# The last stage of a batch, done chunk by chunk inside the scan stage of the next batch

## The reference

```
# layer 0: dilated convolutions, batch norm, relu, then linear attention over the N = 16384 pixels
out = gamma * (msum * tailor)                 # per batch: a 17-row matrix u, and out = G^T u

# layer 1, with x_hsi the output of layer 0
xz = x @ W_in; xh, z = split(xz)              # 128 -> 2 x 256
xh = silu(causal_conv_k2(xh, conv_w, conv_b))
dt_low, Bmat, Cmat = split(xh @ W_x)          # 8 + 16 + 16
dt = softplus(dt_low @ W_dt + b_dt)
h  = exp(dt * A) * h + dt * B * x             # a scan over the pixels, 256 x 16 states
y  = (sum_n h * C + xh * D) * silu(z)
x  = y @ W_out                                # back to 128 channels: "o" below
x  = silu(group_norm(x, gamma, beta))         # 4 groups of 32 channels, over the whole image
return x + x_hsi
```

## Time and profile before

| | us |
|---|---|
| median of 3 runs (16718.77 to 16725.19) | 16720.4 |
| the profiled execution, its own time | 16713.74 |
| its span, first to last instruction | 16712.0 |
| busy: PE / DVE / ACT / POOL | 14237.2 / 14036.9 / 9963.5 / 13059.7 |
| granted TensorE clock, mean | 0.912 |

### The profile page before, as it was taken

One profiled execution on the slowest core, in us unless ns is written; L12 is line 12 of the kernel. 1 busy time (PEld: TensorE's weight loads), 2 busy tenths in 40 slices (PEclk: granted clock), 3 DMA queues, 4 the chain that ended last, 5 costly groups with the idle time before them and its releaser, 6 DMA issues. The chain is left out here.

```text
span 16712.0 us, 141790 instructions
## 1 busy us (share of the span) xinstructions
PE 14237.2 (85%) x40250; PEld 5369.3 (32%) x40250; DVE 14036.9 (84%) x13540; ACT 9963.5 (60%) x13655; POOL 13059.7 (78%) x5647
## 2 busy tenths in 40 slices
PE   8999988888888888888888888888888888888876
PEld 3333333333333333333333333333333333333322
DVE  1222229999999999999999999999999999999942
ACT  2222226666666666666666666666666666666631
POOL 0000009999999999999999999999999999999930
PEclk9999988999999999999999999999999999999965
DMA  1111104444444444444444444444444444444455
GB/s 49 42 44 38 39 27 167 166 169 169 166 169 169 169 166 166 166 167 162 167 168 169 169 166 169 169 166 169 167 167 162 166 167 167 169 169 167 168 194 211
DMA packets 508713, 2504.88 MB, mean 150 GB/s; under 512 B 53097, under 2 KB 164938, under 8 KB 226651
## 3 DMA queue, kind: packets, MB, share of 16 engines
q1 hardware_dynamic: 489723, 2419.71, 40.0%
q10 hardware_dynamic: 18208, 76.11, 1.2%
HBM read 2325.05 MB, written 170.57 MB: 149 GB/s over the span
## 5 line engine op out<-in xcount | busy, mean ns | idle before, releaser
L728 POOL TENSOR_TENSOR hc<-h,c_all 128x1024 f32<-128x1024 f32 x4096 | 9523.5, 2357 | 458.0 <-DVE h L1043 441.6
L940 PE MATMUL y_ps<-hc,ident 128*128 128x512 f32 x16392 | 8513.9, 665 | 1436.1 <-POOL hc L728 1434.1
L824 ACT ACTIVATE d_a<-dt,a_neg 128x512 f32<-128x512 f32 x8194 | 5594.9, 689 | 4215.2 <-DVE h L1043 4205.6
L1043 DVE TENSOR_TENSOR_SCAN h<-d_a,h,dbx_v 128x512 f32<-128x512 f32 x5456 | 6623.6, 1262 | 8.8
L940 PEld LDWEIGHTS y_ps<-hc,ident 128*128 128x128 f32 x16392 | 3304.4, 211 | 6533.9 <-issue 3802.1
L1030 DVE TENSOR_TENSOR dbx_v<-dtx_ps,b_all 128x1024 f32<-128x1024 f32 x2816 | 3316.3, 1208 | 60.3 <-DMA b_all<-bc_dram 24.4
L1043 DVE TENSOR_TENSOR_SCAN h<-d_a,h,dbx_p 128x512 f32<-128x512 f32 x2480 | 3024.4, 1261 | 0.0
L717 POOL TENSOR_TENSOR dbx_p<-dtx,b_all 128x1024 f32<-128x1024 f32 x1280 | 3000.2, 2353 | 25.0 <-DVE h L1043 2.0
L479 POOL MEMSET ident_f<- 128x128 f32 x1 | 0.2, 204 | 2416.7 <-POOLq L44 2416.7
L272 PE MATMUL conv_ps<-image,w_taps 128*32 128x512 f32 x11520 | 1778.8, 595 | 0.0
L362 DVE RECIPROCAL k_inv<-k_nrm 128x4 f32<-128x4 f32 x256 | 45.5, 178 | 1776.0 <-ACT k_nrm L214 1776.0
(11 more groups left out here) (123 smaller groups left out, 8958.7 us busy)
## 6 DMA issues: line engine op xcount, KB each, us to landing
b_all<-bc_dram SPq DMA_DIRECT2D x1028, 1024.0 KB, 6.3
c_all<-bc_dram SPq DMA_DIRECT2D x1025, 1024.0 KB, 4.8
o_dram<-o_sb SPq DMA_DIRECT2D x257, 256.0 KB, 5.6
o_t<-o_dram SPq DMA_DIRECT2D x64, 1024.0 KB, 11.0
out<-r_t ACTq DMA_DIRECT2D x64, 1024.0 KB, 9.2
image<-in_x SPq DMA_DIRECT2D x91, 512.0 KB, 4.0
un<-un_dram SPq DMA_DIRECT2D x516, 34.0 KB
bc_dram<-low_bc SPq DMA_DIRECT2D x257, 64.0 KB, 4.7
```

What stands on the lines that cost most here:

```text
L728: nc.gpsimd.tensor_tensor(hc[:, n % HC], h[:, n], c_all[:, n // CG % 2, n % CG].unsqueeze(1).broadcast_to([128, 2, CH]), ALU.mult).then_in ...
L824: nc.scalar.activation(d_a[:, half], dt[:, p, half], ACT.Exp, scale=a_neg[:, half, n:n + 1]).then_inc(a_done, 1)
L940: last = nc.tensor.matmul(y_ps[:, half], ident[:], hc[:, n % HC, half], start=False, stop=(n == S - 1))
L1043: nc.vector.tensor_tensor_scan(h[:, n, half], d_a[:, half], dbx, zero_col[:] if first else h[:, n, half, CH - 1:CH], ALU.mult, ALU.add).th ...
```

## The change

In the scan stage, chunk `km` now also does the last stage for chunk `u = km - 34` of all (chunk 0 is the first of batch 0): TAIL_LAG = NCH + 2 chunks behind. This is done for u = 0 to 219. What is left for `phase_c` are 36 chunks: nine blocks of 2048, the last of batch 6 and the eight of batch 7.

For each of the 220 chunks ("tail") there are added: on SP a load of `o_c` (256 KB) and of 17 rows of `u_c` (34 KB), issued one chunk ahead, and a store of `r_c` (256 KB), one chunk behind; on ACT `silu_tail` behind `silu_z`, with the same table, and `copy_tail` behind `copy_out`; on PE two matmuls (G^T u with 17 rows, and an identity matmul that adds `o_c`) behind `out_product`, into `p_ps[:, 0]`. `u_c` and `gm_c` are partitions 64 to 80 of the tiles `un` and `w_xz`.

For each of 7 batches there are added, in its second chunk or just before it: three small DVE operations at the end of `aggregate`, one 128 x 2 matmul `share_out` with the group matrix, three small DVE operations `variance`, a square root on ACT (`deviation`), and four small DVE operations `scale_shift`.

`phase_c` now has four buffers for `o_t` and `r_t`, reads scale, shift and matrix in place, lets PE and ACT go two blocks ahead of DVE, and puts the four matmuls of a block on four different groups of 32 rows of the array.

```
+TAIL_LAG = NCH + 2
+TAILS = B * NCH - NCH - SUB
+def tail_of(km):
+    u = km - TAIL_LAG
+    return u if 0 <= u < TAILS else None

 SP:
+            def load_tail(u):
+                at = u // NCH, u % NCH * CH
+                after(sp, "tail_mm", u - 1)
+                after(sp, "o_stored", 16 * (u + 2))
+                sp.dma_start(o_c[:, u % 2], o_dram[:, (u + 1) * CH:(u + 2) * CH]).then_inc(tail_in[u % 2], 16)
+                c0 = (at[0] * SLOTS + 1) * CH + at[1]
+                sp.dma_start(u_c[:, u % 2], un_dram[:, c0:c0 + CH]).then_inc(tail_in[u % 2], 16)
+            def store_tail(u):
+                after(sp, "tail_copied", u + 1)
+                sp.dma_start(out[u // NCH, :, u % NCH * CH:u % NCH * CH + CH], r_c[:, u % 2]
+                             ).then_inc(tail_stored[u % 2], 16)
             def body(b, km, un_at, p, last):
                 after(sp, "z_mm1", km + 1)
                 load_un(un_at, p)
+                if tail_of(km - 1) is not None:
+                    store_tail(tail_of(km - 1))
+                if tail_of(km + 1) is not None:
+                    load_tail(tail_of(km + 1))
...
                 if last:
-                    sp.dma_start(w_xz[:], ...
+                    sp.dma_start(w_xz[0:K2], ...

 ACT:
+            def deviation(b):
+                after(act, "var_done", b)
+                nc.scalar.activation(g_std[:], g_var[:], ACT.Sqrt, bias=gn_eps[:]).then_inc(std_done, 1)
+            def silu_tail(u):
+                after(act, f"tail_in{u % 2}", 32 * (u // 2 + 1))
+                after(act, "scaled", 4 * (u // NCH + 1))
+                nc.scalar.activation(o_c[:, u % 2], o_c[:, u % 2], ACT.Silu, bias=shifts[:, bt:bt + 1],
+                                     scale=scales[:, bt:bt + 1]).then_inc(tail_silu, 1)
+            def copy_tail(u):
+                after(act, "tail_mm", u + 1)
+                after(act, f"tail_stored{u % 2}", 16 * (u // 2))
+                nc.scalar.activation(r_c[:, u % 2], p_ps[:, 0], ACT.Copy).then_inc(tail_copied, 1)

 PE:
+            def share_out(b, km):
+                after(pe, "st_done", 3 * b)
...
+                nc.tensor.matmul(p_ps[:, 0, 0:2], share[:], st[:], start=True, stop=True).then_inc(share_mm, 1)
+            def tail(u, dts):
...
+                after(pe, "tail_silu", u + 1)
+                nc.tensor.matmul(p_ps[:, 0], gm_c[:, u // NCH % 4], u_c[:, u % 2], start=True, stop=False)
+                nc.tensor.matmul(p_ps[:, 0], ident[:], o_c[:, u % 2], start=False, stop=True).then_inc(tail_mm, 1)

 DVE, end of aggregate, then behind weigh(km, 1), then ahead of statistics:
+                    nc.vector.tensor_copy(st[:, 0:1], mean_var[:, 0:1]).then_inc(st_done, 1)
+                    nc.vector.tensor_tensor(st_sq[:], mean_var[:, 0:1], mean_var[:, 0:1], ALU.mult)...
+                    nc.vector.tensor_tensor(st[:, 1:2], st_sq[:], mean_var[:, 1:2], ALU.add).then_inc(st_done, 1)
+            def variance(b):
+                after(dve, "share_mm", b)
+                nc.vector.tensor_copy(g_mv[:], p_ps[:, 0, 0:2]).then_inc(g_copied, 1)
+                nc.vector.tensor_tensor(g_sq[:], g_mv[:, 0:1], g_mv[:, 0:1], ALU.mult).then_inc(var_sq, 1)
+                nc.vector.tensor_tensor(g_var[:], g_mv[:, 1:2], g_sq[:], ALU.subtract).then_inc(var_done, 1)
+            def scale_shift(b):
+                nc.vector.reciprocal(g_inv[:], g_std[:]).then_inc(scaled, 1)
+                nc.vector.tensor_scalar(scales[:, at], g_inv[:], gn[:, 0:1], None, ALU.mult)...
+                nc.vector.tensor_tensor(g_off[:], g_mv[:, 0:1], scales[:, at], ALU.mult)...
+                nc.vector.tensor_scalar(shifts[:, at], g_off[:], -1.0, gn[:, 1:2], ALU.mult, ALU.add)...

 phase_c, PE:
+            for b, j, k in blocks:
+                pe.wait_ge(u_in[part_of[k] % 2], 16 * groups * (part_of[k] // 2 + 1))
+                if k >= 2:
+                    pe.wait_ge(added, k - 1)
+                for g in range(groups):
+                    last = nc.tensor.matmul(res_ps[:, k % 2, CH * g:CH * g + CH], gm[32 * g:32 * g + KU, b],
+                                            u_t[32 * g:32 * g + KU, part_of[k] % 2, j], start=True, stop=True)
```

More of the change, by code:

```diff
@@ L38 @@
 CB = 2048
+CBUF = 4
 NCB = N // CB
@@ L566, in phase_b @@
         mark = sb("mark", [C, 1])
+        o_c = sb("o_c", [C, 2, CH])
+        r_c = sb("r_c", [C, 2, CH])
+        share = sb("share_b", [C, C])
+        gn = sb("gn_b", [C, 2])
+        gn_eps = sb("gn_eps_b", [C, 1])
+        st = sb("st", [C, 2])
+        st_sq = sb("st_sq", [C, 1])
+        g_mv = sb("g_mv_b", [C, 2])
+        g_sq = sb("g_sq", [C, 1])
+        g_var = sb("g_var", [C, 1])
+        g_std = sb("g_std_b", [C, 1])
+        g_inv = sb("g_inv", [C, 1])
+        g_off = sb("g_off", [C, 1])
+        scales = sb("scales", [C, B])
+        shifts = sb("shifts", [C, B])
+        u_c = un[64:64 + KU]
+        gm_c = w_xz[64:64 + KU].rearrange("k (s c) -> k s c", c=C)
         d_a = ps("d_a", [128, 2, CH])
@@ L699, in _ @@
             after(sp, "c_in1", 16 * 2 * B * NCH)
+            after(sp, "gm_in", 16 * (B - 1))
+            for s in range(2):
+                after(sp, f"tail_stored{s}", 16 * (TAILS // 2))
         @block.gpsimd
@@ L865, in body @@
                 copy_out(km)
+                if tail_of(km) is not None:
+                    copy_tail(tail_of(km))
                 decay(km, 13, 0, p)
@@ L906, in gated @@
                 after(pe, f"xh_silu{half}", km + 2)
[L907 removed]
+                nc.tensor.matmul(p_ps[:, 1 - half], w_xz[0:K2, DI + 128 * half:DI + 128 * half + 128], un[0:K2, p],
                                  start=True, stop=True).then_inc(z_mm[half], 1)
@@ L985, in body @@
                 out_product(km, km + 2)
+                if tail_of(km) is not None:
+                    tail(tail_of(km), km + 2)
                 add_state(km, 8)
@@ L1072, in body @@
                 weigh(km, 1)
+                if b > 0 and c == 1:
+                    variance(b)
                 run_scan(km, 0, 0, first)
@@ L1163, in phase_c @@
         added = sem("C_added")
-        stored = [sem(f"C_stored{p}") for p in range(2)]
+        stored = [sem(f"C_stored{s}") for s in range(CBUF)]
         block = ctx.enter_context(nc.Block())
+        parts = [(B - 2, NCB - 1), (B - 1, 0)]
+        blocks = [(b, j) for b, j0 in parts for j in range(j0, NCB)]
+        blocks = [(b, j, k) for k, (b, j) in enumerate(blocks)]
+        first_of = [sum(NCB - j0 for _, j0 in parts[:i]) for i in range(len(parts) + 1)]
+        part_of = [i for i, (_, j0) in enumerate(parts) for _ in range(j0, NCB)]
+        groups = CB // CH
         @block.sync
@@ L1201, in _ @@
-            for p in range(2):
-                act.wait_ge(stored[p], 16 * (B * NCB // 2 + 1))
+            act.wait_ge(step, STEPS_BEFORE_USE)
+            for b, j, k in blocks:
+                act.wait_ge(o_in[k % CBUF], 16 * (k // CBUF + 1))
+                if k >= 2:
+                    store(*blocks[k - 2])
+                nc.scalar.activation(act_t[:, k % 2], o_t[:, k % CBUF], ACT.Silu, bias=shift[:, b:b + 1],
+                                     scale=scale[:, b:b + 1]).then_inc(silu_done, 1)
@@ L1204, in _ @@
+            store(*blocks[-2])
+            store(*blocks[-1])
+            for s in range(CBUF):
+                act.wait_ge(stored[s], 16 * len([k for _, _, k in blocks if k % CBUF == s]))
         @block.tensor
```

174 lines of the change are left out of this document (101 added, 73 removed).

## The result

| | before | after |
|---|---|---|
| median of 4 runs each, us | 16721.6 | 16274.7 (16262.7 to 16290.9) |
| the profiled execution, its own time | 16713.7 | 16276.2 |
| scan stage, first to last row of its window | 13504 | 13628 |
| last stage | 679 | 115.9 |

The ratio is 0.9733, 95% interval 0.9721 to 0.9745: faster by 447 us, where the forecast of 16250 meant 471 (16721.6 - 16250). The time is 25 us above the forecast and inside its range, but the terms behind it were further off than that, in opposite directions.

A forecast was written before the change was run, and what follows sets the result against it. DVE, 99% busy, bounds the scan stage; the last stage runs PE and DVE in turn, no engine full. - 607 + 44 + 12 + 83 = - 468 from 16713.7 gives 16246, stated as 16250; 8-in-10 range 16135 to 16400.

The forecast's parts named there:

- last stage: Nine blocks left in `phase_c`: 72 us instead of 679, between DMA bound 57 and PE bound 82; gain 607.
- the worst end that I gave: Last stage: 115 us if each of the nine blocks kept the old step of 10.37 us.
- Their transfers are 9 x (1.05 in + 1.05 out) = 18.9 MB: Last stage: the nine blocks' transfers at 417 GB/s take 45 us; with the head, a DMA bound of about 57.
- The copy at state 13: Scan stage, each of 220 chunks: `copy_tail` on ACT delays state 13's decays, 0.2 us each, 44 in all.
- The silu at state 6: Scan stage, each chunk: `silu_tail` on ACT, 0.68 us, just fits the 0.72 slack before state 6's scan; cost 0.
- The 1.2 + 1.3 us add up: Batch ends: `w_xz` queues behind three tail DMAs, their issue and transfer adding 2.5; 2 us taken for each of 6, 12 in all.
- End of `aggregate`: Each batch: copy `st` and `st_sq` each wait for POOL's running instruction, so scans start 4.9 us later.
- `scale_shift` and `variance`: Each batch's small DVE operations: `scale_shift` meets three POOL operation ends, 5.7 us; `variance` 1.0 us.
- I take the same for the others: Batches' small DVE operations: all wait for POOL's running instruction as the copy seemed to, 0.17 to 2.3 us each.
- Rival 1: Scan-stage additions cost next to nothing, nine blocks at their DMA bound: 16117, or 16150 with half the batches' cost; chance 0.22.
- Rival 2: ACT's added silu and copy delay DVE fully, or the copy waits for late PE: 16549; chance 0.12.
- Rival 3: PE becomes the scan stage's bound: 18030 with half its passes at the low clock, so slower; chance 0.03.

The follow-up runs named there:

- e4: Changed kernel with each 17-row load of the last stage split into 16 rows and 1 row: 16238.5 us, ratio 0.971.
- e5: Changed kernel with the loads of `o_t` for the first four blocks issued ahead of the small ones, 17-row loads left whole: 16280.0 us, a single run.
- e6: Kernel with split 17-row loads, but all four matmuls of a last-stage block read partitions 0 to 16, one row group: 16252.3 us, a single run.
- e3: Changed kernel with `copy_tail` moved from behind `copy_out` to just ahead of the decays of state 15: 16257.1 us, ratio 0.9721.
- e1: Changed kernel with the load of `w_xz` at a batch's end issued ahead of the tail's store and loads: 16257.7 us, ratio 0.9721.
- e2: Changed kernel with `st_sq`, `st`, `g_off` using one tensor input and a per-partition scalar, moments copied as two single columns: 16248.6 us, ratio 0.9714.
- e8: Changed kernel with all mends together, plus `g_sq` and `g_var` in one-input form behind state 0's first scans and `w_xz` split 48 + 1: 16110.9 us, ratio 0.9635.

## Why the prediction was right, and where it was not

| term, us | predicted | measured |
|---|---|---|
| last stage | - 607 | - 563 |
| middle chunks | + 44 (0.2 each) | + 32 (202 x 0.158) |
| batch ends | + 12 (2 each) | + 47 |
| batches' small operations | + 83 (11.8 each) | + 48 (7 x 6.8) |
| sum | - 468 | - 436; the profiled executions differ by 437.5 |

Two terms were too favourable by 79 us together, two too dear by 47, so the total missed by 32 of 468. The prediction's 0.96 for "faster" was safe either way; its 25 us of error was luck in part.

1. **Last stage: mis-sized.** 115.9 us stand at the worst end that I gave (115), but that end was for the old step of 10.37 us per block, which is gone. (By the prediction's own terms it is 12 + 9 x 10.37 + 6 = 111, so 115 was added up wrongly.) The step that failed is "Their transfers are 9 x (1.05 in + 1.05 out) = 18.9 MB", divided by 417 GB/s. It counted the large loads and took the small ones as free. They hold 1.1 MB, but run at 26 GB/s, and the large ones wait behind them. e4 shows it (66.6 us, inside my 57 to 82), e5 that the order isn't it. That one term hid another error which would have gone the other way: 72 stood for a PE at 0.50 that speeds up. PE didn't (e6), but the row groups made it irrelevant. For four groups of rows the Trainium skill (TensorE: Matmul & The Clock Gate, "Why this matters for your kernels") has 3.07 times, which I cited and didn't follow; the trace agrees, with 7.16 to 2.09 us, 3.4 times.
2. **The copy at state 13: right in mechanism and place.** 0.2 predicted; 0.17 net of the gate, of which e3 takes away 0.15. That the gate gives it back can't be seen: its wait varies more than that between runs.
3. **The silu at state 6: right, just.** The silu lasts 0.81 us, but part of it overlaps its neighbours: the slack of decay (6, 0) was 0.76 and is 0.09, so 0.67 of it went, where 0.68 were predicted.
4. **`w_xz`: right place, a quarter of the price.** "The 1.2 + 1.3 us add up" was the step: it took the delay of the transfer for the delay of the gate. PE's wait did grow by 2.8 us, but behind it the clock was 0.50, and twelve slower matmuls added 4.0; the eight ahead of it, slower as well, added 1.35. That makes the 8.2 at the gate. e1 undoes the delay, and 6.0 of the 7.8 us per batch end go with it.
5. **End of `aggregate`: right sum (4.9, measured 4.6), wrong operations.** The 4.6 run from the start of the copy `st` to the scans, 7 times alike. I let the copy `st` and `st_sq` wait; it was `st_sq` and the sum, with two inputs, for 2.31 and 2.27, and the one-column copy took 0.14. The Trainium skill (GPSIMD Engine Reference, "8. Key points") names two SBUF inputs as one case of the conflict; the trace agrees, and e2 takes the wait away with the input. My extrapolation from the copy was the wrong way to get there: the copy of two columns has one input and takes 1.43 beside POOL, two copies of one column 0.15 each.
6. **`scale_shift` and `variance`: too dear, 5.7 and 1.0 against 1.15 and 0.48.** With the 4.6 this is 6.2 of the 6.8 us that a batch's first two chunks are longer; the rest was not traced. The same step, "I take the same for the others": operations with one tensor of one column do not wait, so of three waits for POOL one was left (`g_off`, 0.55).
7. **Rivals.** Rival 1 (almost free) isn't the change as it stands, but e8 is near it: with +6 in the scan stage it takes 16111, where rival 1 said 16117 (16123 with the 6.7 us between the profiled execution and the median, which the forecast adds and rival 1 left out). Rival 2 would need chunks longer by 1.36; they are by 0.16. Rival 3 would need a clock that falls; it stayed at 0.92.

## What to carry to other kernels

Price a load by its number of rows before its bytes: 17 rows ran at a sixteenth of the bandwidth, held up the queue behind them for 48 us, and 16 + 1 cured it. A wait in front of PE costs more than its length if the clock falls behind it: here 2.8 us more of waiting brought 4.0 more in the matmuls that followed. And small DVE operations beside a busy POOL are cheap if they read a single tensor of one column and use a per-partition scalar for the other operand: 0.2 us against 2.3.

## What the hardware showed that I had not expected

- Loads of 17 rows at 22 to 32 GB/s for 40 us, and SP blocked in the issue of the next ones, 31.81 us for four.
- PE's clock stayed at the lower of its levels, 0.50, for 54.97 us of matmuls without a gap, all on 17 rows (e6); in the scan stage, on 128 rows, it was 0.92 on average. What in these matmuls makes the difference was not tried.
- A one-column copy of 0.15 us (e2) and a two-column copy of 1.43 us, both beside a busy POOL.
- DVE's wait at the gate of the middle chunks differs by up to 0.19 us per chunk between kernels whose order there is alike. Its cause stays open.
